# The last stage of a two-layer convolution kernel: units of 16 rows, four landing slots per stream, the relu's result in PSUM, one queue for every transfer

## The reference, cut to what matters

```python
q1 = ternary_quantize(w1)
out1 = relu(batchnorm(conv3x3(x, q1), gamma1, beta1))      # x: group norm of x1
q2 = ternary_quantize(w2)
out2 = batchnorm(conv3x3(out1, q2), gamma2, beta2)
return relu(out1 + out2)                                   # the caller adds x1 to it
```

## Time and profile before

| | |
|---|---|
| median of three runs | 3130.37 us |
| the profiled execution, its own time | 3130.63 us |
| its span in the profile | 3129.0 us |
| last matrix multiplication of the convolution part ends | about 2934.5 us |
| first instruction of the last part (L943) | 2942.6 us |
| last store issued (L911) | 3122.4 us |

### The profile page before, as it was taken

The page is one execution under the profiler, slowest core; times in us unless marked ns, Lnnn a source line. Parts: engine busy times, 40 slices in busy tenths (PEclk is TensorE's granted clock), DMA queues, the critical chain, the costliest instruction groups (busy, mean ns, idle before and its releaser), DMA issues. The chain is left out here.

```text
span 3129.0 us, 40030 instructions
## 1 busy us (share of the span) xinstructions
PE 2624.7 (84%) x11674; PEld 1748.8 (56%) x11674; DVE 2243.4 (72%) x6010; ACT 1207.7 (39%) x2103; POOL 1331.4 (43%) x1294
## 2 busy tenths in 40 slices
PE   4768888888999999899899999998998969999500
PEld 2434444445655566565565555555555769999500
DVE  5478888888878878888788878778875246666544
ACT  1234343444444444544344444434442123323244
POOL 1045555554554555445455555555550013333111
PEclk9788999999999999999999999999999989999755
DMA  5579999998999998989899998999993211111387
GB/s 158 175 265 343 346 335 337 336 355 290 329 334 334 347 341 321 320 301 337 295 330 333 332 320 314 330 325 336 326 323 119 70 55 57 57 49 58 114 278 252
DMA packets 286852, 827.53 MB, mean 264 GB/s; under 512 B 26204, under 2 KB 59996, under 8 KB 285924
## 3 DMA queue, kind: packets, MB, share of 16 engines
q0 software_dynamic: 170496, 620.83, 55.0%
q1 hardware_dynamic: 116196, 204.94, 19.9%
HBM read 740.19 MB, written 85.48 MB: 264 GB/s over the span
## 5 line engine op out<-in xcount | busy, mean ns | idle before, releaser
L360 POOL DMA_INDIRECT G<-pixel_pairs,quad_c x1152 | 1145.8, 995 | 1009.6 <-PE psT L783 724.7
L646 DVE SCALAR_TENSOR_TENSOR G<-G,wts_c 128x256 f32<-128x256 f32 x3456 | 1407.3, 480 | 211.5 <-ACT G L408 203.8
L746 PE MATMUL psD<-ST,wconv 128*128 128x512 f32 x2304 | 1073.3, 612 | 0.0
L746 PEld LDWEIGHTS psD<-ST,wconv 128*128 128x128 f32 x2304 | 436.3, 199 | 455.2 <-issue 455.2
L735 PE MATMUL psF<-pf,qw 128*128 128x512 f32 x2304 | 631.5, 423 | 14.6 <-DVE pf L570 7.6
L408 ACT ACTIVATE G<-G,wts_c 128x256 f32<-128x256 f32 x1152 | 507.5, 500 | 190.9 <-DMA G<-pixel_pairs,quad_c 153.5
L735 PEld LDWEIGHTS psF<-pf,qw 128*128 128x128 f32 x2304 | 429.3, 189 | 163.6 <-issue 54.7
L783 PE MATMUL psT<-idn,G 128*128 128x128 f32 x2304 | 326.8, 288 | 188.4 <-DVE G L646 188.4
L445 ACT ACTIVATE ST<-psT 128x1024 f32<-128x1024 f32 x288 | 293.7, 1020 | 437.4 <-PE psT L783 437.3
L783 PEld LDWEIGHTS psT<-idn,G 128*128 128x128 f32 x2304 | 279.3, 148 | 267.8 <-issue 133.4
L735 PE MATMUL psA<-po,woff 128*64 128x512 f32 x1152 | 349.8, 452 | 6.3 <-DVE po L570 6.3
(11 more groups left out here) (137 smaller groups left out, 1652.6 us busy)
## 6 DMA issues: line engine op xcount, KB each, us to landing
pixel_pairs<-yT SPq DMA_DIRECT2D x112, 256.0 KB, 5.3
G<-pixel_pairs,quad_c POOLq DMA_INDIRECT x1152, 6.3
xz<-in_x SPq DMA_DIRECT2D x32, 512.0 KB, 6.1
xres<-in_x SPq DMA_DIRECT2D x32, 512.0 KB, 7.1
x<-x1c SPq DMA_DIRECT2D x32, 512.0 KB
h<-h1c SPq DMA_DIRECT2D x32, 512.0 KB, 3.9
area<-h SPq DMA_DIRECT2D x32, 512.0 KB, 6.8
area<-x SPq DMA_DIRECT2D x32, 512.0 KB, 5.3
```

Of the source, the lines that this page charges most:

```text
L360: pool.indirect_dma_start(out=G[:, i % RING, :], out_offset=None, in_=tbl[d.b].rearrange("y x q c -> (y x) (q c)"), in_offset=bass.Indirec ...
L646: dve.scalar_tensor_tensor(g[:, 0:C], g[:, q * C:(q + 1) * C], wts_c[:, d.p, q * NG + i:q * NG + i + 1], g[:, 0:C], ALU.mult, ALU.add).the ...
L746: ins = pe.matmul(psD[:, oc, :], wconv[:, t, k, oc * 128:(oc + 1) * 128], ST[:, k % 3, t, :], start=(k == 0 and t == 0), stop=(k == TAPS - ...
```

## The change

A unit of the last part has EU = 2 * PX = 1024 pixels, 16 rows; there are NEU = 16 units, and every transfer is 1 MB in contiguous rows of 4 KB. h1 and x1 have ESLOTS = 4 landing slots each: in `area`, `own`, `po` and `qw`, tiles of the convolution part that are free after it. Slot 0 (`area`) is loaded at the last `g_split` as before, slots 1 to 3 when TensorE has ended (`g_conv`). `relu1` writes to PSUM (`ps_r1`, a view of `psG`, two buffers) and not over the landed h1, and `mix` reads it there. So an h1 slot is free when its relu is done. The stores are issued by SyncE, each behind the loads of the unit four further on. GpSimd has nothing to do in this part.

```diff
-            h1w, x1w = (area[:, i * CT * PX:(i + 2) * CT * PX].rearrange("p (s x) -> p s x", s=2) for i in (0, 2))
+            EU, ESLOTS = 2 * PX, 4
+            NEU = NCH * PX // EU
+            own_flat = own[:].rearrange("p n r w -> p (n r w)").bitcast(F32)
+            po_f, qw_f = po_flat.bitcast(F32), qw[:].rearrange("p t k o -> p (t k o)").bitcast(F32)
+            land = [[r[:, i * CT * EU:(i + 1) * CT * EU].rearrange("p (t x) -> p t x", t=CT) for r in (area, own_flat, po_f, qw_f)]
+                    for i in range(2)]
+            h1w, x1w = land
+            ps_r1 = psG[:].rearrange("p q t j x -> p q t (j x)")
...
-                hold(sp, g_split, NCH + CR)
-                with sp.Fori(0, NCH // NR) as j:
-                    for u in range(NR):
-                        b, r = j, u
-                        hold(sp, e_mac, NR * j + u - 1 + CR)
-                        sp.dma_start(h1w[:, u % 2, :].rearrange("p (t x) -> p t x", t=CT), rows_of(h1_d, b, r * RC, RC)).then_inc(e_lh[u % 2], 16)
-                        hold(sp, e_sum, NR * j + u - 1 + CR)
-                        sp.dma_start(x1w[:, u % 2, :].rearrange("p (t x) -> p t x", t=CT), rows_of(x1_d, b, r * RC, RC)).then_inc(e_lx[u % 2], 16)
+                def store_out(j, v):
+                    hold(sp, e_sum, ESLOTS * j + v + 1 + ESLOTS)
+                    sp.dma_start(rows_of(out, j, v * (EU // W), EU // W), h2[:, :, ds((ESLOTS * j + v) * EU, EU)]).then_inc(e_st, 16)
+                def load_unit(j, v):
+                    hold(sp, e_r1, CT * (ESLOTS * j + v - ESLOTS + 1) + CT * ESLOTS)
+                    sp.dma_start(h1w[v], rows_of(h1_d, j, v * (EU // W), EU // W)).then_inc(e_lh[v], 16)
+                    hold(sp, e_sum, ESLOTS * j + v - ESLOTS + 1 + ESLOTS)
+                    sp.dma_start(x1w[v], rows_of(x1_d, j, v * (EU // W), EU // W)).then_inc(e_lx[v], 16)
+                sp.sem_inc(e_r1, CT * ESLOTS)
+                sp.sem_inc(e_sum, ESLOTS)
+                sp.wait_ge(g_split, NCH + CR)
+                load_unit(0, 0)
+                sp.wait_ge(g_conv, NCH + CR)
+                for v in range(1, ESLOTS):
+                    load_unit(0, v)
+                with sp.Fori(0, NEU // ESLOTS - 1) as j:
+                    for v in range(ESLOTS):
+                        load_unit(j + 1, v)
+                        store_out(j, v)
+                for v in range(ESLOTS):
+                    store_out(NEU // ESLOTS - 1, v)
+                sp.wait_ge(e_st, 16 * NEU)
...
-                with pool.Fori(0, NCH // NR) as j:
-                    for u in range(NR):
-                        hold(pool, e_sum, NR * j + u + 1 + CR)
-                        pool.dma_start(rows_of(out, j, u * RC, RC),
-                                       h2[:, :, ds((NR * j + u) * PX, PX)]).then_inc(e_st, 16)
-                hold(pool, e_st, 16 * NCH)
...
+                    def relu1(v):
+                        act.wait_ge(e_lh[v], 16 * (j + 1))
+                        act.wait_ge(e_mac, ESLOTS * j + v - 1 + CR)
                         for t in range(CT):
-                            v = h1w[:, u % 2, t * PX:(t + 1) * PX]
-                            act.activation(v, v, ACT.Relu, bias=bias_b[:, 0, t:t + 1], scale=scale_b[:, 0, t:t + 1]).then_inc(e_r1, 1)
+                            act.activation(ps_r1[:, v % 2, t], h1w[v][:, t], ACT.Relu,
+                                           bias=bias_b[:, 0, t:t + 1], scale=scale_b[:, 0, t:t + 1]).then_inc(e_r1, 1)
...
+                            h = h2[:, t, ds((ESLOTS * j + v) * EU, EU)]
+                            i = dve.scalar_tensor_tensor(h, h, scale_b[:, 1, t:t + 1], ps_r1[:, v % 2, t], ALU.mult, ALU.add)
```

More of the change, by code:

```diff
@@ L864, in build @@
             g_part, g_h, g_stat = (sem2(n) for n in ("g_h2_begun", "g_h2", "g_stats"))
-            e_lx = [sem2(f"e_x1_loaded{i}") for i in range(2)]
-            e_lh = [sem2(f"e_h1_loaded{i}") for i in range(2)]
+            e_lx = [sem2(f"e_x1_loaded{i}") for i in range(ESLOTS)]
+            e_lh = [sem2(f"e_h1_loaded{i}") for i in range(ESLOTS)]
             e_st = sem2("e_out_stored")
@@ L937, in _, with relu2 @@
                 act.wait_ge(g_bn, 2)
-                with act.Fori(0, NCH // NR) as j:
-                    def relu1(u):
-                        act.wait_ge(e_lh[u % 2], 16 * (NR // 2 * j + u // 2 + 1))
+                with act.Fori(0, NEU // ESLOTS) as j:
+                    def relu1(v):
+                        act.wait_ge(e_lh[v], 16 * (j + 1))
+                        act.wait_ge(e_mac, ESLOTS * j + v - 1 + CR)
                         for t in range(CT):
-                            v = h1w[:, u % 2, t * PX:(t + 1) * PX]
-                            act.activation(v, v, ACT.Relu, bias=bias_b[:, 0, t:t + 1], scale=scale_b[:, 0, t:t + 1]).then_inc(e_r1, 1)
-                    def relu2(u):
-                        act.wait_ge(e_mac, NR * j + u + 1 + CR)
+                            act.activation(ps_r1[:, v % 2, t], h1w[v][:, t], ACT.Relu,
+                                           bias=bias_b[:, 0, t:t + 1], scale=scale_b[:, 0, t:t + 1]).then_inc(e_r1, 1)
+                    def relu2(v):
+                        act.wait_ge(e_mac, ESLOTS * j + v + 1 + CR)
                         for t in range(CT):
-                            v = h2[:, t, ds((NR * j + u) * PX, PX)]
-                            i = act.activation(v, v, ACT.Relu, bias=bias_b[:, 1, t:t + 1], scale=1.0)
+                            h = h2[:, t, ds((ESLOTS * j + v) * EU, EU)]
+                            i = act.activation(h, h, ACT.Relu, bias=bias_b[:, 1, t:t + 1], scale=1.0)
                         i.then_inc(e_r2, 1)
                     relu1(0)
[L952 to L955, removed]
+                    for v in range(1, ESLOTS):
+                        relu1(v)
+                        relu2(v - 1)
+                    relu2(ESLOTS - 1)
             @block2.vector
@@ L1017, in batch @@
                             planes(chunk(b + 1, r + AHEAD - NR))
-                for ready in (g_v, g_h, e_mac, e_sum):
+                for ready in (g_v, g_h, e_mac):
                     dve.sem_inc(ready, CR)
@@ L1026, in _, with mix, add_x1 @@
                 batch_norm(1, bn2_stats)
-                with dve.Fori(0, NCH // NR) as j:
-                    def mix(u):
+                with dve.Fori(0, NEU // ESLOTS) as j:
+                    def mix(v):
                         for t in range(CT):
-                            dve.wait_ge(e_r1, CT * (NR * j + u) + t + 1)
-                            v = h2[:, t, ds((NR * j + u) * PX, PX)]
-                            i = dve.scalar_tensor_tensor(v, v, scale_b[:, 1, t:t + 1], h1w[:, u % 2, t * PX:(t + 1) * PX], ALU.mult, ALU.add)
+                            dve.wait_ge(e_r1, CT * (ESLOTS * j + v) + t + 1 + CT * ESLOTS)
+                            h = h2[:, t, ds((ESLOTS * j + v) * EU, EU)]
+                            i = dve.scalar_tensor_tensor(h, h, scale_b[:, 1, t:t + 1], ps_r1[:, v % 2, t], ALU.mult, ALU.add)
                         i.then_inc(e_mac, 1)
[L1035 to L1039, removed]
+                    def add_x1(v):
+                        dve.wait_ge(e_r2, ESLOTS * j + v + 1)
+                        dve.wait_ge(e_lx[v], 16 * (j + 1))
+                        h = h2[:, :, ds((ESLOTS * j + v) * EU, EU)]
+                        dve.tensor_tensor(h, h, x1w[v], ALU.add).then_inc(e_sum, 1)
                     mix(0)
[L1041 to L1044, removed]
+                    for v in range(1, ESLOTS):
+                        mix(v)
+                        add_x1(v - 1)
+                    add_x1(ESLOTS - 1)
             @block2.tensor
```

## The result

The changed kernel takes 3048.45 us (median of four runs, 3047.21 to 3052.58) against 3130.62: a ratio of 0.974, 95% interval 0.9723 to 0.9756. The direction and the mechanism held, the size did not.

A forecast was written before the change was run, and what follows sets the result against it. A two-slot ring left the DMA engines idle 20%; with deeper slots their rate binds: 2936.0 plus 130.4 us (48.2 MB at 370 GB/s) plus 3.4 gives span 3069.8, time 3071 us; range 3055 to 3088.

The forecast's parts named there:

- the ring of two slots: Last part before the change: two units per turn, 11.7 us of landing, work and issue, leaving the DMA engines idle 20%.
- loads ahead: Begin of the last part: six loads issued at TensorE's end, about 2934.95 us, where before nothing was issued until 2945.27.
- order in one queue: SyncE's queue: h1 behind a wait for a sum is at most 4.9 us late, covered by 3 queued units; cost nothing.
- The rate: Last part's transfers with a full queue: 370 GB/s taken, so 48.2 MB need 130.4 us.
- the mixture of directions costs something: Within the rate: loads and stores mixed lose some speed, no size given; 370 GB/s taken.
- The end: From the last byte to the end of the span: 3.4 us, kept as before.
- Does the queue run dry?: Last part's begin: work queued until 2955.8 us, first sum at 2952.1, so x1 of unit 4 joins in time.
- Lower rates for the mixture: Rival: memory holds mixed loads and stores at a lower rate, far end 331 GB/s, 3086.6 us; chance 0.17.
- at their limit already: Rival: the DMA engines' idle 20% is waiting inside transfers, 265 GB/s stays, time 3122.8 us; chance 0.03.
- Turning one queue costs: Rival: 32 turns between load and store; slower above 2.1 us each, 3146 us at 2.6; chance 0.01.
- The change does not do what it says: Rival: slots do not run ahead, one unit's landing and work alternate, end near 3131 us; chance 0.02.
- Larger rows pay more than I take: Rival: rate above 415 GB/s, time under 3057 us, gain ending near 3050 as the queue runs dry; chance 0.06.

The follow-up runs named there:

- n: The kernel before with only its stores moved to SyncE's queue, two slots of 512 KB kept: 3130.06 us.
- d: The changed kernel with two landing slots instead of four for each of h1 and x1, units of 16 rows: 3087.17 us, ratio to before 0.9864.
- g: The changed kernel with the six loads of units 1 to 3 held until the relu of unit 0 has run: 3061.91 us, ratio to before 0.9769.
- a: The changed kernel with units of 8 rows and 8 slots for each of h1 and x1, rows of 2 KB: 3060.07 us, ratio to before 0.9772.
- b: The changed kernel with the 16 stores issued by GpSimd on its own queue: 3055.78 us, ratio to before 0.9763.
- c: The changed kernel without 15 of its 16 output stores, so loads alone but for the last unit: 3030.45 us.
- the second measurement: The changed kernel run once more, unchanged: 3052.87 us, ratio to before 0.9758.
- k: The changed kernel with x1 of unit 2 loaded early, when TensorE has ended the last but one chunk: 3052.48 us, ratio to before 0.976.

## Why the prediction was wrong in its size

**The bound before, the ring of two slots: right.** n keeps the ring and keeps the time; d widens the units and not the number, gains half (38 of 75 us), and has holes. The steps "loads ahead" and "order in one queue" held too: g gives 10.1 us for the begin where I had the issues at 2935.0 and 2945.3. Work on a unit was sized within 1.2% for the mix and the add, and ScalarE's relus at 1133 and 1197 ns for my 1200.

**The step that failed is "The rate".** The transfers bound the part, as I had it, but this term was mis-sized: I took 370 GB/s and gave rates above 415 a chance of 0.06. Measured: 415 GB/s, and at that rate 48.2 MB take 116.1 us instead of 130.4. That is 14.2 us of the miss, the largest piece. Alone it makes 3057 us, still inside the range; the end (below) and the early mark carry the time out of it. Two arguments in the step were wrong, and the runs show each. First, I divided GB/s by the share to get the rate of a full queue: 265 at 80% made 331, 329 at 92% made 358, 285 at 86% made 331. A packet in a queue that keeps running dry counts as busy for longer: d divides to 370 and shows 420 where it is full, and 2 KB packets took 93 ns in n, one queue at 75%, against 81 in a's full one. (The 101 ns of the kernel before had a second queue beside them; in b, a second full queue changes nothing for SyncE's 4 KB packets, 152 ns as in the changed kernel, by the queue's rows over 106 us of b and 111 us of the changed kernel, below. What makes the step from 101 to 93 is open.) Of the rows that I divided all but the weights' 406 came out low, at 331 to 380. That gaps are the reason is shown by d for this stage and inferred for the others, the first block above all, which has other traffic.

```profile
q1 hardware_dynamic: 7925, 30.52, 70.9%
...
q1 hardware_dynamic: 11811, 45.50, 101.1%
```

Second, "the mixture of directions costs something": c shows 409 for loads alone against 415 mixed. The two rows that were right were those of big packets, 407 and 406. (GpSimd's packets before hold 3.6 KB, 16.78 MB in 4608, where one contiguous piece of its stores is 2 KB: a packet can hold more than the one piece that I called it ahead of the prediction.) That the packets' size was the reason is wrong for a long stream: in a full queue 2 KB and 4 KB differ by 3% only. At a stream's begin the size may count for more. The 363 GB/s of the earlier trace rows has a full share (1.02), so no gaps explain it; the changed kernel's two loads of 4 KB rows at the same place reach 418, and a, with 2 KB rows, runs at 378 to 399 GB/s from 2938 to 2960 and only later at 401 to 406. Why was not tried.

```profile
2912.00:2914.00 2.00, 2.00 (x19) 2.00 (x18) 0.22 (x1) 0.00 (x0) 0.00 (x0) 1.00 1.02 418
```

**The end.** I kept 3.4 us from the last byte to the end of the span. The fine slices of the last 5.1 us (0.13 us each, from 3040.0) have their last bytes at 3044.2, 0.9 us before the end:

```profile
GB/s 450 450 386 386 482 386 450 386 353 514 418 418 450 353 418 514 386 418 386 353 514 418 418 482 289 321 386 193 193 129 161 96 32 0 0 0 0 0 0 0
```

They thin out from 3043.4 on. The same slices of n, whose stores SyncE issues too, leave 0.8 us (3127.2 to 3128.0), those of b, with GpSimd's stores, 2.1 us (3050.0 to 3052.1): part of the 3.4 us goes with the engine that issues and awaits the last store, and what makes the rest of it is open. From the 135.3 us that I had for the part (3069.8 - 2934.5) the rate takes 14.2 and the end 2.5, which leaves 118.6; the measured 119.6 to 120.1 hold about 1 us more, since the dip and the thin end run below 415 GB/s.

**Ahead of the part.** The other 9 us between forecast and profile are no effect of the change but the mark's scatter, and so luck, against me here. The whole gain of 82 us holds about 75 of the change (194.5 - 119.6), and the second measurement's 3052.87 us lies 2 us below the range.

**Does the queue run dry?** At 370 GB/s I found 2955.8 against a sum at 2952.1; at 415 the margin is used up: the six loads and h1 of unit 4 then last 17.7 us from 2926.6, to 2944.3, and x1 of unit 4 is issued at 2942.97 and brings data about 1 us later. (The sum itself came where I had it, 17.5 us behind the mark for my 17.6.) The changed kernel has its dip to 363 GB/s there (2944 to 2948), and k made the hole plain.

**The rivals.** Lower rates for the mixture (0.17) and "at their limit already" (0.03) fall with the changed kernel's own 415 GB/s. "Turning one queue costs" falls with b (417 GB/s on two queues) and c. "The change does not do what it says" falls with the six issues in 3 us and the full share. The rule of the Trainium skill (DMA: Bandwidth & Descriptors, section Where 436 GB/s comes from) that about 358 GB/s of HBM bind a core's transfers between HBM and SBUF is not borne out by this kernel, which runs on one core: 415 GB/s of loads and stores ran for 106 us. What two cores at once would get, no run here shows. "Larger rows pay more than I take" was the one on the right side; its time, near 3050, came out, but its reason explains 3% of the rate (a against the changed kernel).

## What to carry to other kernels

A rate read where the queue runs dry says little about a queue that doesn't, and dividing it by the busy share doesn't mend that: look for the finest slices in which it is full. For a stage that only streams, count the bytes that are left when the last unrelated engine ends, divide by the full rate, and then check two places by hand, the begin (do the loads that can be issued last until the first unit's work frees a slot?) and the end (is there something left to move while the last unit is worked on?). Depth is to be measured against the work on one unit: four slots of 8 rows hold the full rate in the middle, where two slots of 16 rows, the same memory, don't.

## What the runs showed of the hardware

One queue of SyncE's held 415 to 418 GB/s of mixed loads and stores in rows of 4 KB for 106 us, 402 in rows of 2 KB (transfers of 512 KB), and 420 to 434 in the full slices of rows of 8 KB (2 MB); loads alone 409. Whether the stores had a queue of their own or not did not change the rate (417), only what was left for the end. With a long queue, an issue on SyncE took 1.5 to 2.9 us instead of 0.4, in the changed kernel from 2954.58 on, where a transfer lands 17 to 18 us after its issue; in c, where the DMA engines are as full but loads land after 8 to 12 us, nearly all issues stay at 0.4. It cost nothing here, since the DMA engines were full meanwhile:

```profile
2974.49 1.99 SPq L898 DMA_DIRECT2D po<-h  x1
2976.72 2.71 SPq L900 DMA_DIRECT2D po<-x  x1
2979.79 1.85 SPq L894 DMA_DIRECT2D out<-h  x1
```

Whether these long issues would delay something else that SyncE has to do was not tried.
